# A conditioned feed-forward layer and a generated adapter on one core: new first steps, a first load issued by GpSimd, separated output biases

## The reference

```python
# layer 0, FF = 1024
scale = cond @ norm_w.T + 1.0
h = x * (scale[:, None, :] * rsqrt(mean(x * x, -1) + 1e-6))
val, gate = split(h @ up_w.T, 2)
h = val * gelu(gate)
hq = round(h * 127 / rowmax|h|) / (127 / rowmax|h|)       # 8-bit steps, per row
wq = clip(round(down_w / s), -1, 1) * s                    # s = mean|down_w|
x = hq @ wq.T + x
# layer 1, a different adapter for every sequence
Wd_b = Wd + 0.1 * (cond @ Wdd.T + bdd)                     # 128 x 256
Wu_b = Wu + 0.1 * (cond @ Wdu.T + bdu)                     # 256 x 128
out = x + relu(x @ Wd_b.T + bd) @ Wu_b.T + bu
```

## Time and profile before

| | |
|---|---|
| median of 3 runs | 473.36 us |
| the profiled execution | 473.57 us, with a span of 471.8 us from first to last instruction |
| PE busy | 464.3 us, 98% of the span |
| DVE, ACT, POOL busy | 82%, 77%, 57% |
| chain of waits | 91% PE, 3% DVE, 1% each DMA, ACT, POOL |

### The profile page before, as it was taken

One profiled execution on the slowest core, in us unless ns is written; L12 is line 12 of the kernel. 1 busy time (PEld: TensorE's weight loads), 2 busy tenths in 40 slices (PEclk: granted clock), 3 DMA queues, 4 the chain that ended last, 5 costly groups with the idle time before them and its releaser, 6 DMA issues.

```text
span 471.8 us, 10035 instructions
## 1 busy us (share of the span) xinstructions
PE 464.3 (98%) x3276; PEld 269.3 (57%) x3276; DVE 386.4 (82%) x787; ACT 364.3 (77%) x636; POOL 269.1 (57%) x681
## 2 busy tenths in 40 slices
PE   8999999999999999999999999999999999999996
PEld 7445565665656555555555555555555555655564
DVE  3887798888989898788888887878888888777886
ACT  3788999999999967776777777686686787677664
POOL 1653558565675645465656546656555656544663
PEclk9999999999999999999999999999999999999999
DMA  7925588967778455535545445645535455444343
GB/s 259 392 80 111 135 206 200 260 182 217 182 236 243 104 103 120 106 100 162 130 133 157 91 124 136 166 122 136 137 84 162 124 145 147 113 105 119 101 81 110
DMA packets 118003, 70.99 MB, mean 150 GB/s; under 512 B 102016, under 2 KB 102976, under 8 KB 115904
## 3 DMA queue, kind: packets, MB, share of 16 engines
q1 hardware_dynamic: 117360, 69.63, 56.4%
q10 hardware_dynamic: 592, 0.73, 0.5%
HBM read 37.44 MB, written 8.39 MB: 97 GB/s over the span
## 4 chain that ended last, share of the span: by engine, by line
PE 91%; DVE 3%; DMA 1%; issue 1%; ACT 1%; POOL 1%; ACTq 0%; DVEq 0%; POOLq 0%
PE bank L1147 65%; PE bank L1161 11%; PE bank L1223 5%; PE bank L1255 4%; PE bank L1241 4%; DMA xT_s<-in_xT 1%; PE bank L1123 1%; PE bank L1129 1%; DVE up_lo L1020 0%; ACT gel L621 0%; DVE hid L857 0%; POOL nwt L463 0%; PE bank L1173 0%; DVE amax L865 0%; POOL rms L470 0%
## 5 line engine op out<-in xcount | busy, mean ns | idle before, releaser
L621 ACT ACTIVATE gel<-bank,rms 128x512 f32<-128x512 f32 x125 | 85.5, 685 | 87.3 <-PE bank L1147 84.4
L1147 PE MATMUL bank<-up_hi,xs_hi 128*128 128x512 f16 x492 | 146.3, 379 | 0.3 <-DVE hid L857 0.3
L1147 PE MATMUL bank<-up_lo,xs_hi 128*128 128x512 f16 x492 | 146.3, 379 | 0.0
L1147 PE MATMUL bank<-up_hi,xs_lo 128*128 128x512 f16 x492 | 146.3, 379 | 0.0
L857 DVE SCALAR_TENSOR_TENSOR hid<-bank,rms,gel 128x512 f32<-128x512 f32 x121 | 90.6, 749 | 62.3 <-ACT gel L621 61.5
L1147 PEld LDWEIGHTS bank<-up_lo,xs_hi 128*128 128x128 f16 x492 | 48.1, 98 | 58.1
L1147 PEld LDWEIGHTS bank<-up_hi,xs_lo 128*128 128x128 f16 x492 | 48.1, 98 | 58.0
L448 POOL TENSOR_TENSOR wsplit<-stage,wsplit 128x288 f16<-128x288 f32 x64 | 53.1, 859 | 42.1 <-ACT wsplit L593 42.1
L865 DVE TENSOR_REDUCE amax<-hid 128x1 f32<-128x1024 f32 x61 | 74.4, 1220 | 2.1
L634 ACT ACTIVATE hid<-hid,amax 128x1024 f32<-128x1024 f32 (+1 forms) x62 | 70.0, 1130 | 0.4 <-DVE amax L909 0.4
L1161 PE MATMUL bank<-tern,qT 128*128 128x256 bf16 x504 | 65.3, 273 | 0.8 <-DVE x L969 0.7
(11 more groups left out here) (145 smaller groups left out, 662.7 us busy)
## 6 DMA issues: line engine op xcount, KB each, us to landing
xn_s<-in_xn SPq DMA_DIRECT2D x32, 256.0 KB, 3.4
stage<-in_WddT SPq DMA_DIRECT2D x8, 1024.0 KB, 6.1
stage<-in_WduT SPq DMA_DIRECT2D x8, 1024.0 KB, 5.4
xT_s<-in_xT SPq DMA_DIRECT2D x31, 256.0 KB, 3.1
out<-out_s SPq DMA_DIRECT2D x30, 256.0 KB, 2.3
adapt<-in_up_wT SPq DMA_DIRECT2D x4, 512.0 KB, 7.8
x<-in_down_wT SPq DMA_DIRECT2D x2, 512.0 KB, 9.1
qT<-qn SPq DMA_TRANSPOSE x63, 2.7
```

Source lines behind the costliest of these rows:

```text
L621: nc.scalar.activation(gel_of(t, c), u_banks(t, c)[1][:], ACT.Gelu, scale=rms[:, t // TPB % XN_SLOTS, t % TPB:t % TPB + 1]).then_inc(gelu_ ...
L1147: ins = nc.tensor.matmul(dst[:], a[:, t // TPB % 2, k, cols], w[:, c, k, v, :], start=(k == 0 and n == 0), stop=(k == KD - 1 and n == 2))
```

## The change

Five things, all in the written order of the engines:

1. The first copy of `cond` is loaded by a DMA issued from POOL, ahead of its memsets. SP's first issue is thus the first part of `up_w`. `xT[0]` moves from ACT's queue to SP's, as second issue. `norm_w` has a semaphore of its own.
2. PE multiplies ones 11 and 5 times instead of 8 and 7. In the first half it runs the high passes of both tiles before the low passes of both (`up_first_end`). The sum for the ternary weights moves from before `up(3, 0)` to behind `up(2, 0)`.
3. ACT sums |down_w| and the squares of sequences 2 and 3 earlier; DVE does `ternary_first`, `rsqrt_guess(2)` and `ternary_second` earlier.
4. POOL's `base_sum` moves from between `rsqrt(1)` and `rsqrt(2)` to behind `low_part(0)` in step 5.
5. In the tail, POOL adds the bias to the first tile of sequence 30 earlier and to the second where both stood, and `output(B - 3)` and `total(B - 3)` stand earlier on PE and DVE.

The diff:

```diff
--- before.py
+++ after.py
@@ -69,8 +69,8 @@
 N_NEWTON = 11
-IDLE_FIRST = 8
-IDLE_SECOND = 7
+IDLE_FIRST = 11
+IDLE_SECOND = 5
 LAST_T = NT - 1
@@ -238,6 +238,7 @@
         ld_cond = sem("ld_cond")
+        ld_norm = sem("ld_norm")
         ld_cond_again = sem("ld_cond_again")
         ld_base = sem("ld_base")
         ld_small = sem("ld_small")
@@ -392,9 +393,10 @@
                 i = LAST_ORDER[0]
                 sp.dma_start(out[LAST_B, :, i], late_out[:, i]).then_inc(stored_last, 16)
-            sp.dma_start(cond2[0:C, :], condT).then_inc(ld_cond, 16)
             for n in range(NC * KD):
                 sp.dma_start(raw_up[:, n // KD, n % KD], up_wT[:, n // KD, n % KD]).then_inc(ld_up[n], 16)
+                if n == 0:
+                    sp.dma_start(xT_s[:, 0], xT[0]).then_inc(ld_xT[0], 16)
             sp.dma_start(xn_s[:, 0], xn[0]).then_inc(ld_xn[0], 16)
             load_x(1)
             for i in range(2):
@@ -434,6 +436,7 @@
         @block.gpsimd
         def _(pool):
+            pool.dma_start(cond2[0:C, :], condT).then_inc(ld_cond, 16)
             nc.gpsimd.memset(threehalf[:], 1.5).then_inc(const_ready, 1)
             nc.gpsimd.memset(zero[:], 0.0).then_inc(const_ready, 1)
             nc.gpsimd.memset(cdiag_hi[:], 0.0).then_inc(const_ready, 1)
@@ -511,6 +514,12 @@
                     nc.gpsimd.tensor_tensor(out_s[:, b % OUT_SLOTS, i], x1[:, (b * TPB + i) % X1_SLOTS], bu_row[:], ALU.add
                                             ).then_inc(outb_done, 1)
+            def output_bias_tile(b, i):
+                pool.wait_ge(x1_done, b * TPB + i + 1)
+                pool.wait_ge(stored[b % OUT_SLOTS], 16 * (b // OUT_SLOTS))
+                nc.gpsimd.tensor_tensor(out_s[:, b % OUT_SLOTS, i], x1[:, (b * TPB + i) % X1_SLOTS], bu_row[:], ALU.add
+                                        ).then_inc(outb_done, 1)
+
             def base_sum():
                 pool.wait_ge(ld_base, 16 * N_BASE)
                 nc.gpsimd.tensor_scalar(bias_raw, bias_raw, DELTA_SCALE, None, ALU.mult).then_inc(base_ready, 1)
@@ -520,7 +529,7 @@
                 nc.gpsimd.tensor_scalar(base[:], base[:], A_SCALE, None, ALU.mult).then_inc(base_ready, 1)
             def split_cond():
-                pool.wait_ge(ld_cond, 16 * 2)
+                pool.wait_ge(ld_cond, 16)
                 pool.wait_ge(ld_cond_again, 16)
                 nc.gpsimd.tensor_scalar(cond16[:], cond2[:], C_SCALE, None, ALU.mult).then_inc(cond16_ready, 1)
@@ -545,7 +554,6 @@
             split_cond()
             rsqrt(1)
-            base_sum()
             rsqrt(2)
             for t in range(FIRST - 2):
                 dequantization(t)
@@ -559,6 +567,8 @@
                     low_part(q)
                 for b in scales(s):
                     rsqrt(b)
+                if s == FIRST + 1:
+                    base_sum()
                 if s == LAST_T - 1:
                     residual_low(LAST_T - 4)
                 for b in adapter_splits(s):
@@ -567,11 +577,12 @@
                     identity()
             output_bias(B - 3)
             dequantization(LAST_T - 1)
+            output_bias_tile(B - 2, 0)
             residual_low(LAST_T - 3)
             middle_low(B - 4)
             dequantization(LAST_T)
             residual_low(LAST_T - 2)
-            output_bias(B - 2)
+            output_bias_tile(B - 2, 1)
             middle_low(B - 3)
             pool.wait_ge(x1_lo_done, LAST_T - 2)
@@ -696,8 +707,7 @@
                     nc.scalar.activation(dst, mid_ps[:, 0:S], ACT.Relu, bias=bd_col[:, 0:1],
                                          scale=1.0 / A_SCALE).then_inc(relu_done, 1)
-            act.dma_start(normw, norm_wT).then_inc(ld_cond, 16)
-            act.dma_start(xT_s[:, 0], xT[0]).then_inc(ld_xT[0], 16)
+            act.dma_start(normw, norm_wT).then_inc(ld_norm, 16)
             act.dma_start(cond2[C:2 * C, :], condT).then_inc(ld_cond_again, 16)
             act.wait_ge(const_ready, 2)
             nc.scalar.activation(warm[:], zero[:], ACT.Gelu)
@@ -715,18 +725,18 @@
             squares(0)
             scaled_high(1)
             squares(1)
+            absolute_sum(0)
             gelu(0, 0)
             gelu(0, 1)
             gelu(1, 0)
+            absolute_sum(1)
             gelu(1, 1)
-            absolute_sum(0)
-            absolute_sum(1)
+            squares(2)
             gelu(2, 0)
             quantize(0)
             quantized(0)
             gelu(2, 1)
             scaled_high(2)
-            squares(2)
             gelu(3, 0)
             quantize(1)
             quantized(1)
@@ -738,8 +748,8 @@
                     relu(b)
                 gelu(s, 0)
                 if s == FIRST:
+                    squares(3)
                     gelu(s, 1)
-                    squares(3)
                 quantize(s - 1)
                 if s < LAST_T:
                     for t in split_tiles(s):
@@ -1029,16 +1039,16 @@
             quant_scale(0)
             gate(1, 0)
             gate(1, 1)
+            ternary_first()
             gate(2, 0)
+            rsqrt_guess(2)
             quant_scale(1)
             gate(2, 1)
-            ternary_first()
+            ternary_second()
             gate(3, 0)
-            rsqrt_guess(2)
             scaled_low(2)
             quant_scale(2)
             gate(3, 1)
-            ternary_second()
             ternary_third()
             for s in range(FIRST, NT):
                 if s == LAST_T:
@@ -1083,9 +1093,9 @@
             residual_high_last()
             residual_low(LAST_T)
             residual_low(LAST_T - 1)
+            total(B - 3)
             x63_lo_evacuate()
             x62_evacuate()
-            total(B - 3)
             split_last()
             total(B - 2)
             total_last()
@@ -1098,7 +1108,8 @@
             pe.wait_ge(const_ready, 5)
             idle(IDLE_FIRST)
-            pe.wait_ge(ld_cond, 16 * 2)
+            pe.wait_ge(ld_cond, 16)
+            pe.wait_ge(ld_norm, 16)
             for k in range(KD):
                 ins = nc.tensor.matmul(mid_ps[:, k * B:(k + 1) * B], normw[:, k * P:(k + 1) * P], cond2[0:C, :],
                                        start=True, stop=True)
@@ -1122,6 +1133,10 @@
                         for v, dst in enumerate(u_banks(t, c)):
                             nc.tensor.matmul(dst[:], a[:, 0, k, cols], up_hi[:, c, k, v, :],
                                              start=(k == 0 and n == 0), stop=False)
+
+            def up_first_end(t, c):
+
+                cols = slice(t * P, (t + 1) * P)
                 for k in range(KD):
                     if t == 0:
                         pe.wait_ge(up_ready, c * KD + k + 1)
@@ -1288,15 +1303,20 @@
                 if s < TPB:
                     up_first(0, s)
+                    if s == 1:
+                        up_first_end(0, s)
                     up_first(1, s)
+                    if s == 0:
+                        up_first_end(0, s)
+                    up_first_end(1, s)
                     continue
-                if s == 3:
+                up(s, 0)
+                if s == 2:
                     pe.wait_ge(hid_done, NC + 1)
                     pe.wait_ge(absum_ready, 2)
                     nc.tensor.matmul(sum_ps, ones[:], wsum[:, 0:1], start=True, stop=False)
                     nc.tensor.matmul(sum_ps, ones[:], wsum[:, 3:4], start=False, stop=True).then_inc(absum_full, 1)
-                up(s, 0)
                 for t in downs(s, 0):
                     down(t)
                 if s < LAST_T:
@@ -1320,6 +1340,7 @@
             down_last()
             pe.wait_ge(late_lo_done, 3)
             x_transpose(LAST_T - 2, x61_ps, (0, 1))
+            output(B - 3)
             pe.wait_ge(last_x1_hi_done, 1)
             x_transpose(LAST_T, x63_hi_ps, (0,))
@@ -1328,7 +1349,6 @@
             x_transpose(LAST_T, x63_lo_ps, (1,))
             pe.wait_ge(x1_lo_done, LAST_T - 2)
             x_transpose(LAST_T - 1, x62_ps, (0, 1))
-            output(B - 3)
             middle_last(1)
             middle_last(0)
             output(B - 2)
```

## The result

The changed kernel takes 476.76 us (median of 4 runs, 476.13 to 476.94), the kernel before in the same comparison 473.41 (473.33 to 473.48): a ratio of 1.0069, interval 1.0051 to 1.0086. I had forecast 471.7 and a faster kernel. It is slower by 3.35 us, beyond the range.

What follows compares the result with a forecast made beforehand. PE bounds the kernel, busy 464.3 of 471.8 us, so only the first 50 and last 10 us can gain. Terms −0.40 − 0.30 + 0 − 1.15 + 0.25 − 0.05 = −1.65 on 473.57 give 471.92, median 471.7, range 471.2 to 472.4.

Steps and rivals of the forecast that it cites:

- The tail: Last 10 us: `output(B - 3)` moves into PE's wait of 1.06 at 463.95; −0.05 us, bounds −0.65 and +0.2.
- The clock: PE's ones before about 10 us: the new counts may raise the clock sooner or not; taken as 0.
- Rival B: After 10.1 us PE stays at the lower clock, 0.216 more per 512-column matmul, so the kernel is slower; chance 10%.
- Three gaps: PE's gaps between 36 and 49 us: 0.52 and 0.28 close, 0.89 shrinks to about 0.55; −1.15, bounds 0 and −1.69.
- `base_sum`: Step 5 on POOL: the moved sum makes `low_part(1)` 0.7 to 0.8 late for PE; +0.25, bounds 0 and +1.0.
- Order of the first half: PE from 10.60 to 15.22 us: eight matmuls put ahead remove the wait for `up_lo`; −0.30, bounds 0 and −0.61.
- Loads: Start of the kernel: `up_w` issued earlier, so PE's third part starts earlier by 0 to 0.64; taken as −0.40.
- POOL's DMA and the ones: Start: POOL's issue delays the ones by about 1 us, but `xs_hi` does not decide; 0, ends −0.1 and +0.5.

Runs made afterwards that it cites:

- e2: The kernel before, with only POOL's early bias tile for the first tile of sequence 30 added, the second staying in place: 477.67 us, ratio 1.0094.
- e3: The changed kernel with the early bias tile kept, but sequence 30's output in a buffer of its own, so no wait for a store: 471.26 us, ratio 0.9960.
- e12: The changed kernel with 12 matmuls of ones put into PE's pause ahead of `output(B - 4)`: 474.88 us, ratio 1.0035.
- e7: The kernel before with only the new order of PE's first half (`up_first_end`): 472.80 us, ratio 0.9990.
- e9: As e3, but without the new loads and with the old 8 and 7 ones: 471.96 us, ratio 0.9974 to the kernel before.
- e10: The kernel before with only the new loads, the ones staying 8 and 7: 474.55 us, ratio 1.0023.
- e6: The kernel before with the new loads and 11 and 5 ones: 474.08 us, ratio 1.0021.
- e5: The changed kernel with its whole tail put back (bias tiles, `output(B - 3)`, `total(B - 3)`), leaving only the new head: 472.15 us, ratio 0.9982.
- e1: The changed kernel with only POOL's bias tiles of sequence 30 put back where they stood: 471.70 us, ratio 0.9976.
- e4: The changed kernel with 20 matmuls of ones put into PE's pause ahead of `output(B - 4)`: 475.43 us, ratio 1.0048.
- e8: The kernel before with only the new orders of the first steps on ACT, DVE and POOL, including late `base_sum`: 472.14 us, ratio 0.9974.

## Why the prediction was wrong, point by point

*The tail*, a term of −0.05 with bounds −0.65 and +0.2: +4.56, and it decides everything. The failed step is "It needs POOL's `middle_low(B - 3)`, which one bias (0.7) earlier ends at about 463.1". I counted the moved bias as an instruction of 0.7, with no wait of its own, and left out the wait on `stored` written in its second line, and what stands behind it: `middle_low(B - 4)`, one `output` earlier than the one I looked at. The rows would have given the number. Two tiles at 461.71 and a store issued at 458.54, 2.3 long, say that the slot is free at about 460.9. The change put the tile in front of the instruction that POOL starts at 457.88, so it must wait for 3 us, and PE's `output(B - 4)`, which began at 459.35, waits with it. e2 shows the term alone (+4.63 in *end*), e3 that it is the wait. So the mechanism was wrong, not only the size: the moved instruction brought a wait for a store, and the path to the end ran through `output(B - 4)`, which the sum does not name.

*The clock*, a term of 0. Rival B named a late rise in the head. The price per matmul (0.216 for 512 columns; here 0.1 for 256) was right, but the place was the tail, where a pause of 3.5 brought the clock down for some 3 us: 1.67 (e12).

*Three gaps*, −1.15: 1.15 measured (*middle* 33.15 to 32.00), by the mechanism forecast. `gelu(4, 0)` starts at 34.42 (34.2 forecast), no longer behind POOL. The first four `down` start 3.46, 3.46 and 3.92 apart, and the work between them takes 0.87 + 2.59, 3.46. So the gaps of 0.52 and 0.28 closed and the last is 0.46 (0.55 forecast); 0.1 went at `gate(2, 0)`, as feared.

*`base_sum`*, +0.25: 0. POOL's and PE's timelines of after:

```profile
54.96 2.81 POOL L451 TENSOR_TENSOR wsplit<-stage,wsplit 128x288 f16<-128x288 f32 x4
```

```profile
57.94 0.19 PE L1238 MATMUL bank<-cdiag_hi,wsplit 128*128 128x64 f16 x1
```

`low_part(1)` starts 0.7 late, as forecast (55.79 before, less the head's 1.55, is 54.24). But its four parts took 2.81 instead of 3.07, so they ended at 57.77, 0.17 ahead of PE. The delay was right, and that it cost nothing hung on 0.2 us.

*Order of the first half*, −0.30: 0.29 to 0.31 in the traces (4.62 to 4.33 in e7, 4.31 in e9), as forecast; −0.47 by the medians of e7 (interval 0.05 to 0.9).

*Loads*, −0.40: 0.10 in the trace of after, where PE's first pass on part 2 starts at 10.50 instead of 10.60. With the order *start* is 14.82 instead of 15.22, little more than half of the 0.70 forecast for both. In the six kernels with this head that pass starts at 9.73 to 10.70, so the term is not settled. Alone the loads cost 1.1 (e10), and with the ones no median shows a gain (e6). The step that failed in this term is that part 2 of `up_hi` sets PE's third part. It started at 8.05 (9.49 before, 9.1 forecast), 1.44 earlier, but nobody waited for it: PE began its first real matmul at 9.32, later than before, behind the ones and `cond`. `scaleT` came at 8.21 instead of 6.09, and `xs_hi` and `xs_lo` behind it.

*POOL's DMA and the ones*, 0 from "I take 1" for the issue: the issue holds POOL until 2.03 and the first ones begin at 2.55, 1.27 late, near what I took. But the term was not nothing: with the longer first stretch of ones it took up what the earlier `up_hi` offered. PE's timeline of after:

```profile
2.55 5.06 PE L1107 MATMUL bank<-ones 128*128 128x128 f32 x22 [2.55 <-POOL ones L444]
7.54 0.63 PE L1114 MATMUL bank<-cond,x 64*128 64x32 f32 x4
8.10 1.38 PE L1107 MATMUL bank<-ones 128*128 128x128 f32 x10
9.32 0.59 PE L1134 MATMUL bank<-up_hi,xs_hi 128*128 128x512 f16 x2
```

The clock rises by 7.6 and not at 10, so rival B's own place held no loss.

The head in sum: 1.60 forecast without the tail, 1.55 found in the trace, 1.1 to 1.5 by the medians of e5 and e1. That the two sums are so near is in part luck, since the loads brought 0.3 less and `base_sum` cost 0.25 less than forecast. Without the one line the kernel would have been near the forecast of 471.7. That e1 meets it exactly (471.70) is luck too: its *start* is 0.5 shorter than that of e5, which has the same head, the tail of before and a median of 472.15.

## What to carry to other kernels

An instruction that is moved takes its waits with it. Look up when each semaphore it waits on really fires before you take its duration for its cost, and read who waits for what is queued behind it. On an output slot the time to compare is the store's landing, not its issue or the end of its data's computation, and what stands ahead of the store in its issuer's list counts as well. Here a buffer of its own for the last tiles bought the early place. When PE stands still for some us, add to the pause what the next matmuls lose at the lower clock: here 1.67 on top of 3.14 (after and e12 against e3).

## What the runs showed of the hardware that I had not expected

The moment at which the clock rises differs between executions of the same instructions. Six kernels share the head of after; their first 22 records of ones take 4.26, 4.51, 4.55 and three times 5.06 us, and *start* lies between 14.05 and 15.02. PE's timelines of e4 and of e3, with the short stretches:

```profile
2.56 4.26 PE L1107 MATMUL bank<-ones 128*128 128x128 f32 x22 [2.56 <-POOL ones L444]
6.75 0.63 PE L1114 MATMUL bank<-cond,x 64*128 64x32 f32 x4
```

```profile
2.55 4.55 PE L1107 MATMUL bank<-ones 128*128 128x128 f32 x22 [2.55 <-POOL ones L445]
```

These two and e1 ran on one chip, the three long ones in other comparisons, so by themselves they don't tell the chip from the execution. But e7 and e8 ran on the same chip in the same comparison, and they are equal up to here. Their second stretches of ones, e7 first:

```profile
5.86 1.83 PE L1097 MATMUL bank<-ones 128*128 128x128 f32 x14
```

```profile
5.98 3.35 PE L1098 MATMUL bank<-ones 128*128 128x128 f32 x14
```

The same 14 records ran at the higher clock in one and at the lower in the other. So one profiled execution can't tell differences under 1 us in the head. *Middle*, taken as a distance, repeats within 0.02, and *end* within 0.05 in the seven kernels with the tail of before; e3 and e9, which share their tail, lie 0.19 apart.

The copy of `cond` (8 KB) issued by POOL landed at 6.54, 5.2 us after its issue began; the issue itself kept POOL from its first memset until 2.03 (after; 2.04 in e10). The copy that SP issued first in the kernel before took 2.1. The slow landing is not shown to be POOL's doing: `norm_w`, issued by ACT at 0.8 in both kernels, took 5.3 in after and 2.4 before, and in after a part of `up_w` was issued at 0.8 too. And a pause of 0.8 us in the tail (e12), or of about 1 us (before, at 463.95), left the clock at 1.00, one of 3.5 did not.
